# Layer 0 attention, a two-half software pipeline: the seam between the halves is placed ahead of the chunk matrices instead of behind the masks

## The chip, the cores and the metric

The kernel runs on one core of a Trainium2 chip. The metric is the device time of one execution in microseconds (us). It is one program of several phases; the change touches only the first large one, the attention of layer 0.

## The reference, cut to what matters

```python
x = L0_attn_x                                   # (8, 512, 128): 8 batches of 512 rows
h = _layernorm(x) * (1 + ca) + sa
q, k, v, w = ...                                # 16 heads of 8 channels; w: conv, silu, normed
C = einsum('bhtd,bhsd->bhts', w, w) * beta[:, :, None, :]
L = where(tri_s, C, 0.0) + eye(T)
Rhs = where(tri_s, einsum('bhtd,bhjd->bhtj', w, k), 0.0)
A = solve_triangular(L, Rhs, lower=True, unit_diagonal=True)
qw = where(tri, einsum('bhid,bhtd->bhit', q, w), 0.0)
S = einsum('bhid,bhjd->bhij', q, k) - einsum('bhit,bhtj->bhij', qw, beta[..., None] * A)
logits = S * scale + (G[..., :, None] - G[..., None, :])   # G: cumulative log gate
P = softmax(where(tri, logits, -1e30))
x = x + ga * (einsum('bhij,bhjd->bhid', P, v) @ Wo)
# then: 16 experts, top 4; a second layer of attention and a spiking network
```

The triangular solve is done as products of reflections: within chunks of 16 rows step by step ("distances" 1 to 15), between chunks by one 8x8 matrix per head and chunk.

## The kernel before

**Order of the work.** The attention goes through the 8 batches one after the other. A batch is worked on in two halves. Each of the five engines (SP, POOL, ACT, DVE, PE) has its own `front` and `back` generator, and `weave` merges them at build time: each piece is preceded by a `yield` of a due time in arbitrary units, the piece with the smallest due time is emitted next, and at equal due times `back` goes first. What comes out is a fixed instruction list for each engine, which the engine takes in order; semaphores join the engines. The program has nine stages: the front half of batch 0 alone, seven woven stages (the back half of batch b with the front half of batch b+1, a loop body that is executed seven times), and the back half of batch 7 alone. Between two stages all engines report on `over`, SP clears the semaphores and gives `go` (`close`, L288 to 292).

**Front half, in order.** *Preparation* (due 0 to 44): layer norm, the projections, convolution, sigmoid and silu by Exp, Ln and reciprocal with their table loads on ACT, `qf`, `K0`, `wf`, `bw`, the gate's cumulative sum `gdec`; SP then spreads `gdec` by 16 DMAs into `gshift`. *Distances* d = 1 to 15 (due 50 + 4.5 (d - 1)): DVE makes products `tU`, `tX`, `tS` (L642, L646, L630), PE sums them over a head (L867, L872, L858), DVE multiplies again (L659, L662), POOL subtracts from `K0` and `X2` (L322, L326), on which the next distance waits. *Tokens and chunk matrices* (due 116 to 137): PE transposes `bw` and `X2` (L881, L885), ACT copies them out as `bwt`, `at_even`, `at_odd`; PE builds 14 matrices in four `QUADS` (L896, L901), DVE masks them into `Mk` and `Mq` (L672). *Rolling* (due 139 to 152), n = 1 to 7: three groups of small products on PE (L914, L920, L927), copied out by ACT into `Kr` and `turned_m` (L452, L455) and by DVE into `Rr` (L679); each step needs the one before. *Masks* (due 150 to 158): two more products into `Kx`, then on ACT `aux_l`, four `Kxm`, four `aux_g`, four `Kxm` (L463 to 476), on POOL four `Km` (L343) and `vown`; `vm` on DVE (L685).

**Back half, in order.** *Own block* (due 0 to 3): PE transposes `Sd` (L961), DVE adds the mask into `Sdt` (L692), takes its maximum `mown` (L696), swapped by PE into `mpart`. *Maximum jobs* (due 4 to 44): ten groups of four; PE fills four PSUM banks with scores (L982 with L992 on the diagonal, L986 off it), DVE reduces each bank (L704), and the next group needs the banks. `Qm` on ACT after 16 jobs. *Row maximum and own probabilities* (due 48 to 70): a chain on DVE (L710 to 727) and PE, `Qsm` on POOL (L353), Exp on ACT (L487), then 16 spreads on PE (L1020), each multiplied by DVE (L749) and added by POOL (L365). *Scores* (due 70 to 120): 14 groups of up to three jobs of the 40; PE computes scores (L1033, L1042, L1045), ACT takes Exp (L497), PE multiplies by the values (L1056). *Output* (due 123 to 130): L1074, L1078, L762 to 769, L1084, L1088, L774, L780.

**Buffers.** The front half uses PSUM banks 0 to 3 with its own preparation, distances, matrices and rolling; the back half uses banks 4 to 7. `mats` (14 T columns, T = 512) holds the preparation's temporaries and then the matrices; `Pt`, `oi`, `pv` have memory of their own.

## Time and profile before

| | |
|---|---|
| runs | 3: 3684.28, 3689.19, 3691.18 us; median 3689.19 |
| profiled execution | 3705.26 us, its span 3703.5 us |
| PE busy | 2337.3 us, 63% of the span |
| PE loading weights | 1458.0 us, 39% |
| DVE busy | 1749.8 us, 47% |
| ACT busy | 904.7 us, 24% |
| POOL busy | 875.9 us, 24% |
| mean granted clock of PE | 0.700 of full speed |
| attention of layer 0 | from 66.0 to 2145.9 us |

Times are from the span's start. A line such as L704 is line 704 of the kernel. PE is the engine of matmuls, PEld its weight loads, which lie beside PE. In the rows below, a window row gives the stretch, its length, each engine's busy time with its count of instructions, the granted clock as a share of full speed, and the DMA share and rate. A timeline row gives start, duration, engine, line, operation, the written and read tiles with their shape, the count, and in brackets the idle time before it and what ended that.

### The profile page before, as it was taken

The page shows a single profiled execution, that of the slowest core. Times are in us where ns is not written, and L with a number is a line of the kernel's source. Part 1 is how long each engine was busy: PE and PEld are TensorE (multiplying, and loading weights), DVE is VectorE, ACT ScalarE, POOL GpSimd, SP SyncE. Part 2 cuts the span into 40 slices and gives each one's busy share as a digit, 9 for nine tenths or more (in the row PEclk, how much of TensorE's full clock was granted, in tenths as well). Part 3 has the DMA queues.
Part 4 walks back from the last instruction along what each step waited for, and adds up shares of the span by engine and source line. Part 5 has one row for each costly group of instructions (what it writes and reads, how often), then busy time and mean ns, then how long its engine had stood idle before and what let it go on. Part 6 is the DMA issues. An engine that isn't in the chain of part 4 may idle for free. (4 is left out here: it accounts for less than half of the span.)

```text
span 3703.5 us, 41014 instructions
## 1 busy us (share of the span) xinstructions
PE 2337.3 (63%) x15566; PEld 1458.0 (39%) x15566; DVE 1749.8 (47%) x3402; ACT 904.7 (24%) x1800; POOL 875.9 (24%) x892
## 2 busy tenths in 40 slices
PE   3677878779778778787787852079921133444433
PEld 2353544625525536245255452079920011111111
DVE  4537346264374463652743233023322566766666
ACT  1021231222222312312221210046610222222222
POOL 0404204113032041141230104755567000000000
PEclk7757868759678577587695655589965566666666
DMA  2000000000000000000000050122211100000000
GB/s 74 6 1 6 1 3 4 1 6 1 1 6 1 1 6 1 6 1 1 6 1 1 1 204 30 50 67 71 71 47 49 32 0 0 0 0 0 0 0 23
DMA packets 68043, 72.42 MB, mean 20 GB/s; under 512 B 13906, under 2 KB 57858, under 8 KB 66594
## 3 DMA queue, kind: packets, MB, share of 16 engines
q1 hardware_dynamic: 59682, 53.15, 4.4%
q0 software_dynamic: 8192, 16.79, 1.5%
q8 instruction: 133, 2.18, 0.2%
q14 instruction: 36, 0.29, 0.0%
HBM read 34.83 MB, written 30.93 MB: 18 GB/s over the span
## 5 line engine op out<-in xcount | busy, mean ns | idle before, releaser
L497 ACT ACTIVATE a_Pt<-ps 128x512 f32<-128x512 f32 x320 | 168.6, 598 | 582.7 <-PE ps L1042 436.2
L704 DVE TENSOR_REDUCE a_mpart<-ps 128x4 f32<-128x512 f32 x320 | 202.2, 681 | 176.0 <-PE ps L992 106.2
L1292 ACT ACTIVATE b_hid<-ps,b_stage 128x128 f32<-128x128 f32 x576 | 164.2, 368 | 290.0 <-PE ps L1500 290.0
L982 PE MATMUL ps<-a_aux_g,a_g_hotb 24*128 24x512 bf16 (+1 forms) x320 | 134.9, 540 | 83.1 <-DVE a_mpart L704 79.8
L310 POOL TENSOR_TENSOR a_tS<-a_qf,a_K 128x512 f32<-128x512 f32 x8 | 10.4, 1295 | 729.2 <-DVE a_K L585 729.2
L872 PE MATMUL ps<-a_txy,cst 128*128 128x480 f32 (+14 forms) x480 | 165.8, 476 | 24.8 <-DVE a_txy L646 24.6
L1247 POOL COPY b_stage<-b_w 128x1028 f32 x144 | 150.1, 1043 | 125.2 <-PE ps L1509 125.2
L1857 PE MATMUL ps<-c_num,c_wb 128*128 128x512 f32 x128 | 80.5, 716 | 156.9 <-DVE c_num L1776 156.9
L1411 DVE COPY b_hTp<-ps 128x128 f32<-128x128 f32 x144 | 42.0, 291 | 268.0 <-PE ps L1492 155.6
L322 POOL TENSOR_TENSOR a_K<-a_K,a_yU 128x480 f32<-128x480 f32 (+14 forms) x120 | 83.7, 697 | 358.8 <-DVE a_yU L659 358.8
L326 POOL TENSOR_TENSOR a_X<-a_X,a_txy 128x960 f32<-128x960 f32 (+14 forms) x120 | 149.1, 1242 | 73.1 <-DVE a_txy L662 72.3
L1238 POOL DMA_INDIRECT rows_h<-b_htok,b_slot x128 | 125.8, 983 | 144.3 <-DVE b_slot L1391 102.8
L867 PE MATMUL ps<-a_tU,cst 128*128 128x480 f32 (+14 forms) x240 | 104.9, 524 | 86.9 <-DVE a_tU L642 44.0
L1500 PE MATMUL ps<-b_hTp,b_stage 128*128 128x128 f32 x1152 | 153.3, 276 | 0.0
L1509 PE MATMUL ps<-b_stage,b_hid 128*128 128x128 f32 x1152 | 152.4, 275 | 0.3 <-ACT b_hid L1292 0.3
L1492 PE MATMUL ps<-cst,b_hrow 128*128 128x128 f32 x144 | 40.0, 278 | 176.7 <-DMA b_hrow<-rows_h 176.6
L1845 PE MATMUL ps<-cst,c_xn 128*128 128x128 f32 x64 | 17.8, 433 | 204.8 <-DVE c_xn L1721 204.8
L1257 POOL DMA_INDIRECT b_w<-rows_y,b_slot x128 | 130.7, 1021 | 47.1 <-issue 40.6
L1500 PEld LDWEIGHTS ps<-b_hTp,b_stage 128*128 128x128 f32 x1152 | 141.2, 193 | 0.0
L1509 PEld LDWEIGHTS ps<-b_stage,b_hid 128*128 128x128 f32 x1152 | 140.2, 192 | 0.6 <-ACT b_hid L1292 0.5
L872 PEld LDWEIGHTS ps<-a_txy,cst 128*128 128x128 f32 x480 | 95.4, 226 | 86.4 <-DVE a_txy L646 50.0
L982 PEld LDWEIGHTS ps<-a_aux_g,a_g_hotb 24*128 24x128 bf16 (+1 forms) x320 | 24.7, 97 | 245.2 <-DVE a_mpart L704 210.8
(405 smaller groups left out, 5314.8 us busy)
## 6 DMA issues: line engine op xcount, KB each, us to landing
rows_h<-b_stage SPq DMA_DIRECT2D x9, 1024.0 KB, 10.8
b_hrow<-rows_h SPq DMA_DIRECT2D x144, 64.0 KB, 1.9
rows_y<-b_orow SPq DMA_DIRECT2D x144, 64.0 KB, 1.5
b_w<-in_wexp SPq DMA_DIRECT2D x16, 514.0 KB, 16.7
rows_h<-b_htok,b_slot POOLq DMA_INDIRECT x128, 2.2
b_w<-rows_y,b_slot POOLq DMA_INDIRECT x128
out<-xs SPq DMA_DIRECT2D x1, 2048.0 KB, 8.7
cst<-in_const SPq DMA_DIRECT2D x1, 1865.5 KB, 8.2
```

Of the source, the lines that this page charges most:

```text
L326: nc.gpsimd.tensor_tensor(x, x, yX[:, :, 0:n].rearrange("p a (c s) -> p a c s", c=NC), ALU.subtract).then_inc(e_uX.sem, 1)
L497: nc.scalar.activation(Pt[:, n % (2 * LANES), :], ps[:, 4 + n % LANES, :], ACT.Exp).then_inc(e_exp.sem, 1)
L704: nc.vector.tensor_reduce(mpart[:, i, j, 4 * g:4 * g + 4], ps[:, 4 + n % 4, :].rearrange("p (r j) -> p r j", r=4), AX.X, ALU.max).then_inc ...
L867: mm(ps[:, 0, 0:n], con("block8"), tU[:, 0:n], start=True, stop=True).then_inc(e_pU.sem, 1)
L872: last = mm(ps[:, 1 + a, 0:n], con("block8"), tX[:, a, 0:n], start=True, stop=True)
L982: mm(banks[g], g_hotb[some[g], :], aux_g[some[g], :, keys], start=True, stop=False, skip_group_check=True)
L1238: nc.gpsimd.indirect_dma_start(hrows, bass.IndirectOffsetOnAxis(slot[:, k, n:n + 1], 0), htok[:, n, :], None).then_inc(e_sent.sem, 16)
L1247: nc.gpsimd.tensor_copy(stage[:, p % 3, :], we[:, bass.ds(e, 1), :]).then_inc(e_stage.sem, 1)
L1257: nc.gpsimd.indirect_dma_start(got[:, b % 2, t, k, :], None, yrows, bass.IndirectOffsetOnAxis(slot[:, k, n:n + 1], 0))\
L1292: last = nc.scalar.activation(hid[:, p % 2, f, :], ps[:, p % 2, 128 * f:128 * f + 128], ACT.Gelu, bias=stage[:, p % 3, AT_B1 + f:AT_B1 + f ...
L1500: last = mm(ps[:, q % 2, 128 * f:128 * f + 128], stage[:, q % 3, 128 * f:128 * f + 128], hTp[:, q % 2, :], start=True, stop=True, skip_gro ...
L1509: last = mm(ps[:, 4 + r % 2, 0:D], hid[:, r % 2, f, :], stage[:, r % 3, F + D * f:F + D * f + D], start=f == 0, stop=f == NF - 1, skip_gro ...
```

## The change

The generators are cut at another place. `front` ends with the last distance and `Sd`; tokens, matrices, rolling and masks open `back`. They work in PSUM banks 4 to 7, ahead of the maximum jobs. The own block's transposes, mask, maximum and swap no longer open the half: they are put between the rolling steps n = 1, 2, 4 and 5, and the gate's `aux_l` and `aux_g` on ACT ahead of the copy of step 6. The first group of maximum jobs waits for `aux_g`, `Km` and `Kx` but no longer for all of `Kxm`; the fifth group (the first off the diagonal) waits for `Kxm`.

Due times: a distance every 6.6 units (`DS`) instead of 4.5, rolling at 22 + 2.6 n (`RO`, `RS`), all that was in the back half is 38 later (`BK`). The preparation's due times stay. So within a woven stage the preparation is merged with tokens, matrices and rolling; distances 1 to 6 with the maximum jobs; 7 to 9 with the own probabilities; 10 to 15 with score groups 0 to 11; score groups 12 and 13 and the output have no front piece due beside them.

Memory: the preparation gets `prep` (11 T columns, `sq` and `inv` share), `turned_m` its own; `Pt`, `raws`, `oi`, `pv` move into `mats`; `bwt`, `at_even`, `at_odd` into `shared`. The front half gets waits ahead of writing `vf`, `K0`, `bw`, `X2` and `gspl`, which the back half now still reads; the waits for `e_x`, `e_max`, `e_osum`, `e_mulv` and `e_pv` at its end are gone. A stage is over when the distances are.

The diff, cut to its core (what is left out are bank numbers, 0 to 3 becoming 4 to 7, `BK +` ahead of the back half's other due times, and repetitions of the edits shown):

```diff
+        prep = sb("prep", [128, 11 * T])
+        cut = [prep[:, T * i:T * i + T] for i in range(11)]
+        sq = inv = cut[0:3]
+        conv, esig, gate1, w0, ebeta, gy, gabs, gmin = cut[3:11]
         mats = sb("mats", [128, 14 * T])
-        cut = [mats[:, T * i:T * i + T] for i in range(14)]
-        sq, inv = cut[0:3], cut[3:6]
-        conv, esig, gate1, w0, ebeta, gy, gabs, gmin = cut[6:14]
...
-        turned_m = tS[:, 0, :].rearrange("p (i k f) -> p i k f", i=2, k=2)
+        turned_m = sb("turned_m", [128, 2, 2, 128])
...
-        Pt = sb("Pt", [128, 2 * LANES, T])
+        Pt = mats[:, 0:2 * LANES * T].rearrange("p (n t) -> p n t", t=T)
         on, oT, yg = Pt[:, 1, :], Pt[:, 2, :], Pt[:, 0, :]
-        raws = [shared[:, 7 * T + T * i:8 * T + T * i] for i in range(3)] + [Pt[:, 0, :]]
-        oi, pv = sb("oi", [128, T]), sb("pv", [128, 2, T])
+        raws = [mats[:, 6 * T + T * i:7 * T + T * i] for i in range(4)]
+        oi, pv = mats[:, 10 * T:11 * T], mats[:, 11 * T:13 * T].rearrange("p (a t) -> p a t", a=2)
...
+        e_sdT, e_sdm, e_mi, e_miT, e_mic = ev("sdT", 2), ev("sdm", 2), ev("mi"), ev("miT"), ev("mic")
...
+        DS, RO, RS, BK = 6.6, 22, 2.6, 38
...
+                if over_back:
+                    po.wait_ge(*e_tok(1))
...
-                    yield 50 + 4.5 * (d - 1) + 3
+                    yield 50 + DS * (d - 1) + 3
...
-                yield 119
-                po.wait_ge(*e_uU())
-                po.wait_ge(*e_uX())
-                if over_back:
-                    po.wait_ge(*e_x())
+            def back():
+                yield 0
+                nc.gpsimd.tensor_copy(vown[:, :], vf[:, :]).then_inc(e_vown.sem, 1)
                 nc.gpsimd.tensor_copy(steps_k(), in_steps(K0[:, :])).then_inc(e_diag.sem, 1)
-                if over_back:
-                    po.wait_ge(*e_max())
-                    po.wait_ge(*e_qm())
-                    po.wait_ge(*e_qsm())
                 nc.gpsimd.tensor_copy(steps_q(), in_steps(X2[:, 0, :])).then_inc(e_diag.sem, 1)
-                yield 150
-                if over_back:
-                    po.wait_ge(*e_osum())
                 for r in range(4):
                     nc.gpsimd.tensor_scalar(Km[:, r, :], K0[:, :], con("head_of4")[:, r:r + 1], None,
                                             ALU.mult).then_inc(e_km.sem, 1)
-                if over_back:
-                    po.wait_ge(*e_mulv())
-                nc.gpsimd.tensor_copy(vown[:, :], vf[:, :]).then_inc(e_vown.sem, 1)
-
-            def back(after_front):
-                yield 48
+                yield BK + 48
...
-            po.wait_ge(*e_km())
-            po.wait_ge(*e_vown())
+            po.wait_ge(*e_uU())
+            po.wait_ge(*e_uX())
...
+                if over_back:
+                    act.wait_ge(*e_vown())
+                    act.wait_ge(*e_tok(2))
...
-                yield 120
+            def back():
+                yield 1
                 act.wait_ge(*e_tok(0))
-                act.wait_ge(*e_uX())
-                nc.scalar.copy(bwt, ps[:, 0, :].rearrange("p (t f) -> p t f", t=NT)).then_inc(e_tokc.sem, 1)
+                nc.scalar.copy(bwt, ps[:, 4, :].rearrange("p (t f) -> p t f", t=NT)).then_inc(e_tokc.sem, 1)
...
-                    yield 137 + 2.2 * n
+                    yield RO + RS * n
+                    if n == 6:
+                        act.wait_ge(*e_auxp())
+                        nc.scalar.activation(aux_l[:, :], ps[:, 7, :], ACT.Identity, bias=con("one_rows")).then_inc(e_auxl.sem, 1)
+                        act.wait_ge(*e_auxl())
+                        for r in range(4):
+                            nc.scalar.activation(aux_g[:, r, :], aux_l[:, :], ACT.Copy,
+                                                 scale=con("row_of4")[:, r:r + 1]).then_inc(e_auxg.sem, 1)
                     act.wait_ge(*e_pk(n - 1))
                     nc.scalar.copy(Kr[:, n, :].rearrange("p (t x) -> p t x", x=128)[:, :, 0:C * n],
...
+                yield RO + RS * 7 + 2.5
                 act.wait_ge(*e_kx(0))
-                nc.scalar.copy(Kx[:, 0:2, :], ps[:, 0, 0:256].rearrange("p (n s) -> p n s", s=128)).then_inc(e_kxc.sem, 1)
+                nc.scalar.copy(Kx[:, 0:2, :], ps[:, 4, 0:256].rearrange("p (n s) -> p n s", s=128)).then_inc(e_kxc.sem, 1)
                 act.wait_ge(*e_kx(1))
-                nc.scalar.copy(Kx[:, 2, :], ps[:, 1, 0:128]).then_inc(e_kxc.sem, 1)
-                act.wait_ge(*e_auxp())
-                nc.scalar.activation(aux_l[:, :], ps[:, 3, :], ACT.Identity, bias=con("one_rows")).then_inc(e_auxl.sem, 1)
+                nc.scalar.copy(Kx[:, 2, :], ps[:, 5, 0:128]).then_inc(e_kxc.sem, 1)
                 act.wait_ge(*e_kc())
-                if over_back:
-                    act.wait_ge(*e_osum())
...
-                act.wait_ge(*e_auxl())
-                for r in range(4):
-                    nc.scalar.activation(aux_g[:, r, :], aux_l[:, :], ACT.Copy,
-                                         scale=con("row_of4")[:, r:r + 1]).then_inc(e_auxg.sem, 1)
                 act.wait_ge(*e_kxc())
                 for r in range(4):
...
-            def back(after_front):
-                yield 26
+                yield BK + 26
...
+                if over_back:
+                    ve.wait_ge(*e_diag())
+                    ve.wait_ge(*e_km())
...
+                if over_back:
+                    ve.wait_ge(*e_tok(0))
...
+                if over_back:
+                    ve.wait_ge(*e_auxp())
...
-                yield 118
+                yield 50 + DS * 14 + 7
...
+            def back(gate, tiles):
+                yield 3
+                ve.wait_ge(*e_tok(2))
+                nc.vector.tensor_copy(vm[:, :, 0:DH], ps[:, 6, :].rearrange("p (n c) -> p n c", c=DH)).then_inc(e_vm.sem, 1)
                 for j, (kind, n) in enumerate(BUILD):
-                    yield 122 + 1.1 * j
+                    yield 6 + 1.1 * j
...
-                    yield 137 + 2.2 * (7 - r)
+                    yield RO + RS * (7 - r)
                     w = C * (7 - r)
+                    if r in (6, 5):
+                        h = slice(2 * (6 - r), 2 * (6 - r) + 2)
+                        ve.wait_ge(*e_sdT(6 - r))
+                        nc.vector.tensor_tensor(Sdt[:, h, :], ps[:, 7, :].rearrange("p (t e) -> p t e", e=256),
+                                                con("mask_intra").unsqueeze(1).broadcast_to([128, 2, 256]),
+                                                ALU.add).then_inc(e_sdm.sem, 1)
+                    if r == 4:
+                        ve.wait_ge(*e_sdm())
+                        nc.vector.tensor_reduce(mown[:, :, :], Sdt[:, :, :].rearrange("p t (e h) -> p t h e", h=H),
+                                                AX.X, ALU.max).then_inc(e_mi.sem, 1)
+                    if r == 2:
+                        ve.wait_ge(*e_miT())
+                        nc.vector.tensor_copy(mpart[:, :, 4, :], ps[:, 7, 0:64].rearrange("p (t h) -> p t h", h=H))\
+                            .then_inc(e_mic.sem, 1)
...
-            ve.wait_ge(*e_vm())
+            ve.wait_ge(*e_sd())
+            ve.wait_ge(*e_yX())
...
-                yield 116
+                yield 50 + DS * 14 + 6
                 distance(C - 1)
-                pe.wait_ge(*e_bw())
-                pe.wait_ge(*e_yU())
+            def back():
+                yield 0
                 for t in range(NT):
...
+                for t in range(NT):
+                    last = nc.tensor.transpose(ps[:, 6, 128 * t:128 * t + 128], vf[:, 128 * t:128 * t + 128], con("ident"))
                 last.then_inc(e_tok.sem, 1)
...
-                    yield 121 + 1.1 * done
...
                         pe.wait_ge(*e_tokc())
-                        pe.wait_ge(*e_sd())
+                        pe.wait_ge(*e_vm())
...
-                    yield 137 + 2.2 * n - 1
+                    yield RO + RS * n - 1
                     r = 7 - n
+                    if n in (1, 2):
+                        if n == 2:
+                            pe.wait_ge(*e_sdm(0))
+                        for t in range(2):
+                            for half in range(2):
+                                last = nc.tensor.transpose(ps[:, 7, 256 * t + 128 * half:256 * t + 128 * half + 128],
+                                                           Sd[:, half, 256 * (n - 1) + 128 * t:256 * (n - 1) + 128 * t + 128],
+                                                           con("ident"))
+                        last.then_inc(e_sdT.sem, 1)
+                    if n == 4:
+                        pe.wait_ge(*e_mi())
+                        mm(ps[:, 7, 0:64], con("swap"), mown[:, :, :].rearrange("p t h -> p (t h)"), start=True,
+                           stop=True).then_inc(e_miT.sem, 1)
+                    if n == 5:
+                        pe.wait_ge(*e_mic())
+                        for s in range(3):
+                            mm(ps[:, 7, :], gselb[:, s, :], gspl[:, s, :], start=s == 0, stop=False, skip_group_check=True)
+                        last = mm(ps[:, 7, :], step_selb[:, :], stepb[:, :].unsqueeze(1).broadcast_to([8, NT, 128]), start=False,
+                                  stop=True, skip_group_check=True)
+                        last.then_inc(e_auxp.sem, 1)
                     if n >= 2:
                         pe.wait_ge(*e_kc(n - 2))
...
-                yield 153
-                pe.wait_ge(*e_gsp())
-                for s in range(3):
-                    mm(ps[:, 3, :], gselb[:, s, :], gspl[:, s, :], start=s == 0, stop=False, skip_group_check=True)
-                last = mm(ps[:, 3, :], step_selb[:, :], stepb[:, :].unsqueeze(1).broadcast_to([8, NT, 128]), start=False,
-                          stop=True, skip_group_check=True)
-                last.then_inc(e_auxp.sem, 1)
+                yield RO + RS * 7 + 1.5
...
-            def back(after_front):
-                yield 0
-                if after_front:
-                    pe.wait_ge(*e_auxg())
-                    pe.wait_ge(*e_km())
-                    pe.wait_ge(*e_kxm())
-                    pe.wait_ge(*e_vm())
-                for t in range(NT):
...
-                last.then_inc(e_sdT.sem, 1)
-                yield 2
-                pe.wait_ge(*e_mi())
-                mm(ps[:, 6, 0:64], con("swap"), mown[:, :, :].rearrange("p t h -> p (t h)"), start=True,
-                   stop=True).then_inc(e_miT.sem, 1)
-                pe.wait_ge(*e_sdm())
...
-                    yield 4 + 1.1 * n
+                    yield BK + 4 + 1.1 * n
                     i, _, j = MJOBS[n]
                     keys, blk = slice(128 * j, 128 * j + 128), 128 * i
                     if n == 0:
-                        pe.wait_ge(*e_mic())
+                        pe.wait_ge(*e_auxg())
+                        pe.wait_ge(*e_km())
+                        pe.wait_ge(*e_kxc())
+                    if n == NT * G4:
+                        pe.wait_ge(*e_kxm())
```

## Rows read from the trace of the kernel before

**Rows 1.** Windows (columns in the head line): the first stage, front half alone; then all woven stages.
```profile
core 0: us, PE busy (x) PEld busy (x) DVE busy (x) ACT busy (x) POOL busy (x), PEclk, DMA share, GB/s
66.00:106.20 40.20, 18.23 (x28) 5.92 (x28) 22.27 (x33) 20.68 (x27) 3.80 (x3) 0.65 0.02 5
106.20:174.90 68.70, 47.91 (x120) 23.81 (x121) 37.28 (x77) 0.00 (x0) 30.13 (x30) 0.78 0.02 5
174.90:202.00 27.10, 16.75 (x136) 10.19 (x135) 9.43 (x15) 1.85 (x3) 7.89 (x7) 0.50 0.00 1
202.00:230.00 28.00, 27.94 (x142) 27.81 (x143) 2.93 (x8) 4.95 (x14) 0.00 (x0) 0.55 0.00 1
230.00:240.40 10.40, 2.35 (x14) 1.30 (x12) 0.74 (x2) 7.96 (x16) 0.00 (x0) 0.69 0.00 0
...
240.40:1990.90 1750.50, 1405.15 (x10416) 816.24 (x10416) 863.78 (x1526) 428.33 (x742) 405.59 (x420) 0.74 0.01 3
```

**Rows 2.** Windows: one woven stage cut into six stretches.
```profile
240.40:317.60 77.20, 58.57 (x356) 23.43 (x356) 52.22 (x83) 22.91 (x31) 7.09 (x6) 0.59 0.03 7
317.60:362.00 44.40, 33.59 (x78) 15.05 (x79) 30.78 (x47) 2.07 (x2) 27.21 (x27) 0.87 0.00 0
362.00:423.00 61.00, 57.13 (x680) 34.96 (x681) 23.23 (x55) 20.48 (x39) 15.73 (x22) 0.89 0.01 2
423.00:453.40 30.40, 21.60 (x224) 15.59 (x223) 13.61 (x27) 2.83 (x5) 7.90 (x7) 0.81 0.01 1
453.40:480.00 26.60, 26.60 (x141) 26.59 (x142) 2.63 (x7) 4.84 (x13) 0.00 (x0) 0.57 0.00 1
480.00:490.90 10.90, 2.65 (x16) 1.48 (x13) 1.04 (x2) 8.09 (x17) 0.00 (x0) 0.80 0.01 4
```

**Rows 3.** Windows: the last stage, back half alone.
```profile
1991.20:1997.50 6.30, 2.64 (x12) 2.11 (x13) 3.30 (x3) 0.00 (x0) 0.00 (x0) 0.50 0.00 0
1997.50:2046.40 48.90, 40.78 (x312) 15.69 (x312) 24.84 (x40) 2.56 (x4) 0.00 (x0) 0.50 0.00 1
2046.40:2072.30 25.90, 19.57 (x49) 8.90 (x49) 14.86 (x28) 2.07 (x2) 15.72 (x19) 0.74 0.00 1
2072.30:2133.90 61.60, 59.58 (x632) 31.09 (x632) 2.07 (x3) 21.07 (x40) 0.27 (x1) 0.59 0.01 1
2133.90:2145.90 12.00, 8.03 (x56) 7.28 (x52) 4.18 (x12) 0.58 (x1) 0.00 (x0) 0.78 0.00 0
```

**Rows 4.** Timeline: first instruction of the first woven stage and of the last stage.
```profile
240.42 1.28 ACT L395 ACT_TABLE_LOAD   x1 [0.59 <-SPq L292]
...
1991.25 1.51 PE L961 MATMUL ps<-cst,a_Sd 128*128 128x128 f32 x6 [7.62 <-SPq L296]
```

**Rows 5.** Timeline: distances 7 and 10 of the first stage open; one late rolling step, next piece.
```profile
145.23 0.45 DVE L642 TENSOR_TENSOR a_tU<-a_wf,a_K 128x288 f32<-128x288 f32 x1
...
158.46 1.19 DVE L642 TENSOR_TENSOR a_tU<-a_wf,a_K 128x192 f32<-128x192 f32 x1 [0.20 <-POOL a_K L322]
...
477.75 1.04 PE L914 MATMUL ps<-a_roll_k,a_mats 128*128 128x112 f32 x8
...
479.98 0.81 PE L933 MATMUL ps<-a_gspl,a_gselb 128*128 128x512 bf16 x3
```

**Rows 6.** Timeline: one group of four maximum jobs, its filling and its reduction.
```profile
2020.64 2.48 DVE L704 TENSOR_REDUCE a_mpart<-ps 128x4 f32<-128x512 f32 x4 [2.17 <-PE ps L986]
...
2023.18 2.31 PE L986 MATMUL ps<-a_shared,a_roll_q 32*128 32x512 f32 x8
```

**Rows 7.** Timeline: Qsm on POOL, and a distance on PE that waited.
```profile
314.19 6.16 POOL L353 TENSOR_SCALAR a_shared<-a_roll_q,cst 128x384 f32<-128x384 f32 x4 [10.91 <-DVE a_mpart L704]
...
330.05 1.83 PE L867 MATMUL ps<-a_tU,cst 128*128 128x448 f32 x2 [6.07 <-ACT a_Sdt L490]
```

**Rows 8.** Timeline, PE: the same 24 value products in a woven and in the last stage.
```profile
417.65 0.86 PE L1056 MATMUL ps<-a_Pt,a_values 128*32 128x128 f32 x24
...
2105.17 1.51 PE L1056 MATMUL ps<-a_Pt,a_values 128*32 128x128 f32 x24
```

146 lines of the change are left out of this document (59 added, 87 removed).

## The prediction

> **What bounds the kernel now.** I read windows first, because the chain of waits names only the program's last phase. The change touches only the attention, so I cut that part of the trace where the kernel itself cuts it. The reader is to see three things. The seven woven stages take 1750.8 us, from the first stage's start to the last one's: 250.1 each [rows 4]. The two halves alone are known as well: the front half takes 174.4 us, in five pieces of 40.2, 68.7, 27.1, 28.0 and 10.4 [rows 1]; the back half 154.7, in pieces of 6.3, 48.9, 25.9, 61.6 and 12.0 [rows 3]. Together 329.1, so weaving hides 79.0. And within a woven stage PE is busy for 1405.15 of 1750.5 us, 80% [rows 1]: it is the engine closest to a bound, but half of the stage's stretches are paced by PE, DVE and POOL handing one tile back and forth.
>
> Where weaving hides nothing is plain in the six stretches of a stage: the rolling (26.6 us, DVE 2.63, POOL 0) and the masks (10.9 us, PE 2.65, ACT 8.09) have no partner [rows 2]. These 37.5 us are what the new seam can win. It also takes a partner away from others.
>
> **What moves, and the two ends of the attention.** The first stage loses tokens, matrices, rolling and masks. It ends at 174.9 plus about 1.6 for the last subtractions, `Sd` and the hand-over, instead of at 240.4: minus 63.9. The last stage gains them. Tokens and matrices are 27.1 [rows 1], plus 1.0 for the third set of transposes, which now stands ahead of the matrices. Rolling is 28.0, PE busy 27.94 of it [rows 1], so each PE instruction put between its steps counts in full: 2.64 for the own block's transposes and swap [rows 3] and some 1.4 for the gate's sums (the first three are 0.81 at the faster clock [rows 5]); 32.0. The products for `Kx` are 2.9, the 10.4 of the masks [rows 1] less some 7.5 of ACT's thirteen scalings: the gate's five now lie beside the rolling, the eight `Kxm` beside the first four groups of maximum jobs. That is 63.0, and the 6.3 of the own block [rows 3] is gone from the head: plus 56.7. Both ends together: minus 7.2. The new halves alone are 110.5 and 211.4.
>
> **One woven stage, piece by piece.** I price each piece as the back half's length alone plus what the front's companion adds, and take the share that companions add from the stage of before.
>
> (a) Preparation beside tokens, matrices, rolling, `Kx`. Before, the preparation (40.2 alone) beside own block and maxima (55.2 alone) made a stretch of 77.2 [rows 1 to 3]: it added 22.0, 55%. The same here: 63.0 + 22.0 = 85. Following the lists instead: PE's busy time is 18.2 + 16.8 + 27.9 [rows 1], 4.0 put into the rolling, 1.0 and the `Kx` products, some 69. To it come stalls that the lists force: QUAD 3's last mask stands on DVE behind the reciprocal of `ebeta` (due 20 against 20.3), and PE waits for all masks before it may do the head sums: some 6; the first mask behind `xn`, the normalisation's chain on ACT now behind three copies, PE waiting for masks of QUAD 1, the end of `Kx`: some 8. 83. The gate's scalings put 3.2 us on ACT ahead of the copy of step 6; at 4.0 us for a step on PE [rows 1] that is covered, at the late step's 2.23 [rows 5] one us of it is not. I take 83; bounds 69 (PE alone) and 103 (nothing hidden).
>
> (b) Ten groups of maxima beside distances 1 to 6. Alone 48.9 [rows 3] and 39.0 (distance 7 opens 39.0 after 106.2 [rows 5]). A group is 2.31 of filling, then 2.48 of reduction [rows 6], four banks and no fifth, so the engines alternate already. With a distance in the same lists the next filling waits for reductions that stand on DVE behind `yX`, which waits for PE's `tX` sums. At 55% it is 70; following the lists I get 79, two groups and one distance costing nearly their sum. 75; bounds 49 and 88.
>
> (c) Row maximum and own probabilities beside distances 7 to 9. Alone 25.9 [rows 3] and 13.2 [rows 5]. Before, distances 1 to 5 stood here. Now `Qsm` (6.16 us on POOL [rows 7]) and distance 6's subtractions are due at the same 86.0, and a tie goes to `back`. So distance 6 ends 6 us late, distance 7's products wait for it on DVE, and on PE they stand ahead of the own block's transposes. The trace shows this knot already, PE idle 6.07 us [rows 7]. 36.5; bounds 26 and 39.
>
> (d) 14 score groups beside distances 10 to 15 (16.4 alone [rows 1, 5]). Before, ten distances stood beside them, 61.0 us and some 3 more for the last group, PE busy 57.13 and the clock granted at 0.89 [rows 2]; alone the groups took 61.6 at 0.59 [rows 3]. So PE bounds this stretch, and it is the clock that made the distances look free: the same 24 value products are 0.86 in the woven stage and 1.51 alone [rows 8], the two levels 2.4 and 1.2 GHz. Four distances fewer take some 8 to 11 us of PE away; the last groups, alone now, give back some 3. 56; bounds 50 and 66.
>
> (e) The output, 12.0 [rows 3], stood beside matrices, 30.4 for both and a last group [rows 2]. Now nothing is left of the front half to put beside it: 12.0. Hand-over 0.6.
>
> Sum 263.1, against 250.1: 13.0 more, seven times, plus 91; with both ends plus 84. A check by another road: the new halves together are 321.9, and to stay at 250.1 weaving must hide 71.8 of the shorter one's 110.5, 65%. Before it hid 79.0 of 154.7, 51%, or 58% of the 136.9 of the front half that had a partner. 51% gives 265.5, 58% gives 258. The reason is balance: before, the halves were 174 and 155; now one is twice the other and carries nearly all of the stage as one serial chain. The waits added ahead of `vf`, `K0`, `bw`, `X2` and `gspl` I price at nothing: POOL's copies and four `Km` end some 9 us into the stage, transposes at 3, the gate's sums before the cumulative sum comes again. Without that cover `K0` would hold POOL's `tS` and DVE's list. SP's 16 DMAs are issued once a stage as before and are wanted at distance 9, far later.
>
> The profiled execution, 3705.3, would be 3789; it lies 16.1 above the median of the runs, and the median becomes 3689.2 + 84 = 3773.
>
> **The clock, row against rule.** In the rolling PE is busy without a gap, 26.60 of 26.6 us, and is granted 0.57 on the mean [rows 2], so it stays at 1.2 GHz for most of it. The Trainium skill (TensorE: Matmul & The Clock Gate, Part 1) says that the default state is throttled and that sustained activity releases it; by that rule alone the rolling would already run at 2.4 GHz, which this trace contradicts, since busy with weight loads and narrow products is evidently not enough here. Whether wide products between the steps raise it is the faster rival.
>
> **The rivals.** *The clock rises (faster).* The preparation's 512 column products between the rolling steps, and distances between the maxima, lift (a) and (b) to 2.4 GHz, as the stretch with distances and spreads had 0.87 [rows 2]. A rolling step is then 2.23 [rows 5] instead of 4.0, less ACT's uncovered scalings: 10 off; matrices 6 off; ten fillings at half of 2.31: 11 off. All of it gives a stage of 236 and 3583. It decides from 12.0 of these 27 us, a stage of 251.1. Against it: preparation beside maxima, just such a mixture, had 0.59 [rows 2]. About 20 of the 27 would give 243 and 3632. Chance 0.22. *No change*, a stage of 251 within 1 us, 12 of the 27: 3689. Chance 0.06. *Everything in series*: (a) to (c) at the walked 85, 79, 39, and scores at 62 since fewer distances keep the clock up: stage 278, plus 185, 3874. For it speaks that two groups and a distance already cost their sum in my walk. Chance 0.15. *The forecast* has 0.57, its own range 3725 to 3820.
>
> **How the numbers follow.** Faster 0.22, same 0.06 (within 0.2%, 7.4 us, is about what a measurement of this kernel can tell from no change), slower 0.72. From 3640, which leaves out the deeper half of the faster rival, to 3860, which leaves out the worse half of the serial one.
>
> **What the new profile would show.** The first stage's end near 176; the last stage some 211 long; woven stages of 258 to 268. First maximum group some 83 us into a stage; ten groups lasting 75; `Qsm` and then a late distance 7; output alone on a quiet chip. I am wrong if the granted clock is above 0.75 in the first 160 us of a stage, or if distances slip between maximum groups without delaying the next filling.

## The result, and the profile after

The changed kernel takes 3785.78 us (median of 4 runs, 3775.70 to 3794.14), the kernel before beside it 3689.53 (4 runs, 3684.28 to 3691.18): ratio 1.0262, 95% interval 1.0235 to 1.029. It is slower by 2.6%, 96 us. The profiled execution is 3794.14 us with a span of 3792.3; before it was 3705.26 and 3703.5, some 16 us above that kernel's median, so its stages are up to 2 us longer than usual.

First the windows of the changed kernel: the first two woven stages in five stretches each, the last stage whole, all woven stages together. They answer to [rows 1 to 3].

```profile
core 0: us, PE busy (x) PEld busy (x) DVE busy (x) ACT busy (x) POOL busy (x), PEclk, DMA share, GB/s
176.94:252.40 75.46, 58.61 (x326) 39.18 (x327) 34.64 (x55) 30.85 (x52) 11.72 (x10) 0.67 0.01 4
252.40:325.10 72.70, 53.60 (x360) 24.28 (x360) 46.51 (x73) 6.46 (x12) 14.15 (x10) 0.77 0.02 5
325.10:365.70 40.60, 27.34 (x70) 13.51 (x70) 25.16 (x45) 2.07 (x2) 23.53 (x27) 0.79 0.00 0
365.70:434.50 68.80, 66.62 (x649) 40.11 (x650) 11.35 (x35) 19.90 (x39) 6.68 (x13) 0.58 0.00 1
434.50:448.20 13.70, 8.50 (x87) 6.76 (x85) 4.21 (x13) 1.76 (x4) 0.14 (x1) 1.00 0.01 2
448.20:524.00 75.80, 55.87 (x384) 38.17 (x384) 34.25 (x55) 32.30 (x55) 11.50 (x10) 0.75 0.02 5
524.00:594.80 70.80, 51.88 (x312) 22.85 (x300) 46.52 (x73) 5.01 (x9) 14.19 (x10) 0.76 0.01 4
594.80:635.40 40.60, 27.34 (x70) 13.51 (x70) 25.19 (x45) 2.07 (x2) 23.52 (x28) 0.79 0.00 0
635.40:690.60 55.20, 52.49 (x649) 31.43 (x650) 11.62 (x35) 20.02 (x39) 6.62 (x13) 0.81 0.01 1
690.60:704.10 13.50, 8.37 (x86) 6.68 (x84) 4.18 (x12) 1.63 (x3) 0.10 (x1) 1.00 0.01 2
...
2031.64:2239.10 207.46, 175.56 (x1340) 102.69 (x1340) 61.67 (x109) 40.95 (x79) 23.90 (x27) 0.60 0.00 1
177.00:2031.60 1854.60, 1442.21 (x10416) 833.87 (x10416) 851.80 (x1533) 427.44 (x742) 391.98 (x420) 0.74 0.01 3
```

The stretches are the prediction's (a) to (e). The seven woven stages take 1854.7 us, 264.9 each, against 250.1 [rows 4]: plus 104. The first stage ends at 176.94 and not 240.42, minus 63.5; the last is 207.5 long and not 154.7, plus 52.8. Together the attention ends 93 us later, and that is the whole difference of the two profiled executions, 88.8 us in their spans; the rest of the program is 4.4 us shorter.

The fourth stretch is what nobody would guess from a mean. The first stage has 649 PE instructions in it in 68.80 us, the next has the same 649 in 55.20. Three of the five windows of these stages agree within 0.4 us, and (b) within 1.9, most of which is where the windows are cut; this one is 13.6 apart, and its granted clock is 0.58 and 0.81. The stages' first instructions on any engine (176.97, 448.06, 704.00, 973.67, 1229.63, 1499.33, 1755.30, and 2031.67 for the last stage) give lengths of 271.1, 255.9, 269.7, 256.0, 269.7, 256.0 and 276.4: slow and fast by turns, four slow and three fast. The last one is 6.7 us longer than the other slow ones because its stretch (a) is, 80.9 us for 74.5, at a clock of 0.66 for 0.73: (a) too has more than one length.

Where in the stretch it happens, windows of 8 us show, from the first score product on: those of the first stage, then those of the next.

```profile
365.12:373.12 8.00, 7.42 (x130) 4.83 (x129) 2.21 (x6) 3.15 (x6) 1.91 (x4) 1.00 0.01 2
373.12:381.12 8.00, 7.09 (x61) 4.75 (x58) 1.92 (x5) 1.58 (x3) 0.51 (x1) 0.55 0.00 0
381.12:389.12 8.00, 8.00 (x93) 4.43 (x95) 0.49 (x1) 1.95 (x4) 0.84 (x1) 0.50 0.01 2
389.12:397.12 8.00, 6.99 (x44) 3.75 (x36) 2.89 (x9) 1.20 (x3) 1.17 (x2) 0.50 0.00 0
397.12:405.12 8.00, 8.00 (x70) 5.29 (x71) 0.26 (x1) 3.15 (x6) 0.38 (x1) 0.50 0.01 2
634.80:642.80 8.00, 7.42 (x130) 4.83 (x129) 2.22 (x6) 3.15 (x6) 1.88 (x4) 1.00 0.01 2
642.80:650.80 8.00, 7.09 (x61) 4.75 (x58) 1.92 (x5) 1.58 (x3) 0.51 (x1) 0.54 0.00 0
650.80:658.80 8.00, 7.00 (x105) 3.46 (x103) 1.23 (x3) 3.12 (x6) 0.84 (x1) 0.82 0.01 2
658.80:666.80 8.00, 7.62 (x87) 4.36 (x87) 2.16 (x8) 2.32 (x6) 1.17 (x2) 1.00 0.01 2
```

Up to the second window both are alike to the instruction: the clock falls from 1.00 to half in both. Then it comes back in one and stays at 0.50 in the other. In the third window PE is the busier where the clock stays low (8.00 against 7.00), in the fourth the less busy (6.99 against 7.62); from 397.12 to 429.12 it is busy without a gap, and the clock stays at 0.50. The same 24 value products as in [rows 8] take 0.86 us at 370.89 and 1.51 at 384.01 in the first stage, and 0.86 at 657.13 in the next.

The second thing to see is in stretch (c), in the timeline of the changed kernel's first stage. The columns are start, duration, engine and line, and in brackets the idle time before and who ended it.

```profile
325.12 0.70 DVE L707 TENSOR_REDUCE a_mrow<-a_mpart 128x64 f32<-128x320 f32 x1
325.19 4.91 POOL L344 TENSOR_SCALAR a_shared<-a_roll_q,cst 128x384 f32<-128x384 f32 x4 [6.05 <-DVE a_mpart L701]
328.72 1.06 ACT L479 ACTIVATE a_Sdt<-a_Sdt 128x1024 f32<-128x1024 f32 x1 [41.05 <-DVE a_Sdt L724]
330.06 0.81 POOL L327 TENSOR_TENSOR a_K<-a_K,a_yU 128x320 f32<-128x320 f32 x1
330.91 1.67 DVE L641 TENSOR_TENSOR a_tU<-a_wf,a_K 128x288 f32<-128x288 f32 x1 [2.23 <-POOL a_K L327]
332.64 1.33 PE L866 MATMUL ps<-a_tU,cst 128*128 128x288 f32 x2 [4.42 <-DVE a_tU L641]
336.53 1.04 PE L1006 MATMUL ps<-cst,a_Sdt 128*128 128x128 f32 x8
...
341.17 1.01 ACT L482 COPY a_Sdt<-ps 128x1024 f32<-128x1024 f32 x1 [11.39 <-DVE a_mres L733]
342.32 5.77 PE L1016 MATMUL ps<-a_Sdt,cst 128*128 128x512 f32 x8 [4.75 <-ACT a_Sdt L482]
```

That is the knot of [rows 7] on a longer way. The back half's masks of the own queries (L344) hold POOL; behind them stands distance 6's subtraction (L327); distance 7's product on DVE (L641) and on PE (L866) wait for it; and the back half's own blocks (L1006), whose data ACT had ready at 329.78 (L479), stand on PE behind distance 7 until 336.53. From the row maximum to the first spreading product (L1016) it takes 17.2 us, twice with PE idle for more than 4.

### The profile page after: what moved, and what is told of

It is laid out like the page before. It is cut to its first block and busy times, and to the rows that moved or that the text cites. A ratio compares the mean times of both kernels' runs of the same rounds, so it can differ in the third digit from the quotient of the medians.

```text
span 3792.3 us, 41027 instructions
## 1 busy us (share of the span) xinstructions
PE 2374.1 (63%) x15566; PEld 1476.1 (39%) x15566; DVE 1737.5 (46%) x3410; ACT 904.3 (24%) x1800; POOL 866.4 (23%) x892
## 5 line engine op out<-in xcount | busy, mean ns | idle before, releaser
L489 ACT ACTIVATE a_mats<-ps 128x512 f32<-128x512 f32 x320 | 168.6, 597 | 525.1 <-PE ps L1038 378.7
L327 POOL TENSOR_TENSOR a_K<-a_K,a_yU 128x480 f32<-128x480 f32 (+14 forms) x120 | 83.6, 697 | 697.7 <-DVE a_yU L658 697.7
L1016 PE MATMUL ps<-a_Sdt,cst 128*128 128x512 f32 x256 | 133.9, 673 | 41.2 <-ACT a_Sdt L482 35.9
L866 PE MATMUL ps<-a_tU,cst 128*128 128x480 f32 (+14 forms) x240 | 120.1, 593 | 50.4 <-DVE a_tU L641 49.7
L658 DVE TENSOR_TENSOR a_yU<-a_bw,ps 128x480 f32<-128x480 f32 (+14 forms) x120 | 50.1, 418 | 204.3 <-PE ps L866 204.3
L871 PEld LDWEIGHTS ps<-a_txy,cst 128*128 128x128 f32 x480 | 110.0, 260 | 80.9 <-issue 39.6
## 6 DMA issues: line engine op xcount, KB each, us to landing
rows_h<-b_stage SPq DMA_DIRECT2D x9, 1024.0 KB, 10.8
```

Of the source, the lines that this page charges most:

```text
L489: nc.scalar.activation(Pt[:, n % (2 * LANES), :], ps[:, 4 + n % LANES, :], ACT.Exp).then_inc(e_exp.sem, 1)
L871: last = mm(ps[:, 1 + a, 0:n], con("block8"), tX[:, a, 0:n], start=True, stop=True)
L1016: mm(ps[:, 4 + d % LANES, :], con3("spread", 8)[:, d % 8, :], Pd[:, d // 8, :], start=True, stop=True).then_inc(e_rep.sem, 1)
```

## The experiments

Two theories at first. The forecast's: the loss is that of balance, since one half carries nearly all of the stage as a serial chain; then it comes with where the seam lies and no order of the lists gives it back. The rival: it is what two particular places cost, the knot in (c) and the clock in (d). Each ratio is to runs of the kernel before beside it on the same chip, with its 95% interval. Differences between two experiments are of their medians; their chips are not all the same, and the kernel before took 3688 to 3694 us on them.

**1. A wide product in every score group.**
```diff
+ mm(ps[:, 4 + n % LANES, :], identb[:, :], ident4b, start=True, stop=True)
  some = slice(32 * g, 32 * g + (32 if i == j else 24))
```


> Adds one full-width product (128 x 128 by 128 x 512, its result overwritten at once) ahead of each of the 40 score jobs of a stage; nothing else changes. Theory (the granted clock alone makes the score stretch 68.8 us in one stage and 55.2 us in the next, and it is low because the narrow score and distance products leave the array mostly idle): the granted clock is over 0.85 in the score stretch of every stage, the 271/256 us alternation of stages is gone, the stretch takes 54 to 60 us in all of them though it holds 8.5 us more of products, and the time is 3740 to 3770 us. Rival (the two lengths come from something else, such as where distances and fillings fall against each other, or wide products do not hold the clock): the alternation stays, each stage is 8.5 to 17 us longer, and the time is 3845 to 3900 us.

Measured: 3834.18 us, ratio 1.0407 (1.0383 to 1.043). A window of its score stretch in the first stage (the second's is the same, 70.10 us at 0.90):

```profile
364.20:434.30 70.10, 68.19 (x722) 35.63 (x721) 11.27 (x34) 21.08 (x40) 6.32 (x12) 0.90 0.00 1
```

All seven are so: the turns are gone, as the theory had it. The time is neither theory's, because the added products were mis-priced: from the start of one to the next product on PE it is 346 ns on the mean (13.5 us for 39 of them; their own records overlap the next and are 413 ns long), so forty take 13.9 us, not 8.5. Without them the stretch is 70.1 - 13.9 = 56.2, near the fast 57.0. So the clock makes the difference. Forty wide products cost in a slow stretch what they release, and in a fast one 13 us more.

**2. The order of four steps at the knot.** The own queries' masks go behind distance 6 on POOL, the own blocks ahead of distance 7 on PE and DVE.
```diff
-                yield BK + 48      # POOL, masks of the own queries
+                yield BK + 48.5
-                yield BK + 52      # ACT, exponentials
+                yield BK + 50.5
-                yield BK + 54      # PE and DVE, own blocks
+                yield BK + 51
```


> The changed kernel with four due times moved: GpSimd's masks of the own queries behind distance 6 and not ahead of it, the own blocks' turns and their masks ahead of distance 7, ScalarE's exponentials 1.5 earlier. Theory (the order of the queues around the row maximum makes that stretch 40.6 us where 36.5 was forecast): the stretch from the row maximum to the first score falls to 33 to 36 us, and the time to 3730 to 3760 us. Rival (what this stretch has is TensorE's work at its clock, the order only moves where it waits): 39 to 42 us as now, and 3775 to 3795 us.

Measured: 3678.03 us (9 runs), ratio 0.9972 (0.9962 to 0.9982): 108 us less than the changed kernel, and 0.3% under the kernel before, a difference clear of the noise but small. Both theories are off; the stretch does what the first said, and far more comes with it. Windows of its first stage, (a) to (d), then the seven stages:

```profile
174.96:250.40 75.44, 58.61 (x324) 39.15 (x325) 34.66 (x55) 30.82 (x52) 11.70 (x10) 0.67 0.01 4
250.40:323.15 72.75, 53.61 (x360) 24.30 (x360) 46.52 (x74) 6.47 (x12) 16.14 (x12) 0.77 0.02 5
323.15:358.50 35.35, 27.04 (x70) 13.86 (x70) 23.61 (x45) 2.07 (x2) 21.59 (x27) 0.81 0.00 0
358.50:413.10 54.60, 51.79 (x682) 31.09 (x682) 11.61 (x35) 21.07 (x40) 6.60 (x13) 0.87 0.01 2
...
174.96:1933.30 1758.34, 1375.35 (x10416) 809.80 (x10417) 842.88 (x1533) 428.24 (x742) 391.77 (x420) 0.79 0.01 3
```

(a) and (b) are the same as in the changed kernel's first stage to 0.1 us. (c) is 35.35 instead of 40.60. And (d) is 54.6 at a clock of 0.87, in all seven stages: its slow kind does not occur. A stage is 251.2. But turns remain, in another stretch: (a) is some 75 us in three stages and 78.5 in four. Here are a long and a short one, with 0.70 and 0.75; the first stage has 0.67 and is short all the same, so that the clock makes this difference is not shown.

```profile
673.65:752.25 78.60, 58.44 (x327) 42.02 (x328) 34.46 (x55) 31.06 (x52) 11.60 (x10) 0.70 0.01 4
1431.45:1506.05 74.60, 53.92 (x328) 38.02 (x330) 34.38 (x55) 30.96 (x52) 11.62 (x10) 0.75 0.01 4
```

The seven stages together are 96 us shorter than the changed kernel's: 37 from (c) and 71 from (d), less 12 by which (a) and (b) grew. The timeline of this kernel in (c) shows the own blocks no longer behind the distance:

```profile
327.59 1.97 PE L1006 MATMUL ps<-cst,a_Sdt 128*128 128x128 f32 x8 [1.61 <-ACT a_Sdt L479]
...
332.16 1.30 PE L866 MATMUL ps<-a_tU,cst 128*128 128x288 f32 x2 [2.60 <-ACT a_Sdt L482]
```

The own blocks stand at 327.59, 4.4 us behind the row maximum and not 11.4, and the first spreading product (336.24) comes 13.1 us behind it, not 17.2.

**3. The seam behind the rolling.** Of all that was moved, only masks, auxiliary rows and rotated keys are moved.
```diff
@@ GpSimd, the kernel before
-                yield 150
                 for r in range(4):   # Km, then the copy of v
+            def back(after_front):
+                yield 0
@@ TensorE: gate's sums and the products for Kx
-                yield 153
+            def back(after_front):
+                yield 0
```


> The kernel before with the seam moved the other way: behind the rolling, so that matrices and rolling stay the alone end of the half that prepares, and only the masks, the rotated keys and the auxiliary rows (10.9 us alone) open the half that scores, beside the next stage's preparation. Theory (a part is worth bringing over only as far as it leaves TensorE and the clock room; masks are VectorE's and ScalarE's work beside a stretch that TensorE leaves half idle): 5 to 9 us of each stage's 10.9 are hidden, and the time is 3630 to 3660 us, faster than before. Rival (every item taken over comes back in full as a later end, as the matrices and the rolling did): 3685 to 3700 us. Third (the masks delay the preparation's own copies): 3700 to 3740 us.

Measured: 3660.26 us, ratio 0.993 (0.9913 to 0.9946): 0.7% under the kernel before, at the edge of the theory's 3630 to 3660. A stage is 245.0 (1715.05 us for seven), 5.1 less than before:

```profile
227.59:1942.64 1715.05, 1402.35 (x10416) 812.64 (x10416) 864.77 (x1526) 428.27 (x742) 405.70 (x420) 0.76 0.01 3
```

**4. The seam between matrices and rolling.**
```diff
-        DS, RO, RS, BK = 6.6, 22, 2.6, 38
+        DS, RO, RS, BK = 5.7, 2, 2.6, 20
@@ TensorE: tokens, then matrices, stay in front(), in banks 0 to 3
-            def back():
-                yield 0
+                pe.wait_ge(*e_bw())
+                pe.wait_ge(*e_yU())
...
-                    yield 5 + 1.1 * done
+                    yield 141 + 1.1 * done
```


> The changed kernel with the seam between the matrices and the rolling: tokens and matrices (27 us alone) stay at the end of the half that prepares, as in the kernel before, and the rolling and the masks open the half that scores; offsets are set anew for it (distances 5.7 apart, the back half's dues 18 earlier). Theory (the loss comes of the tokens and matrices: they share TensorE and VectorE with the preparation's products, and push all fifteen distances' partner behind them; the rolling has idle engines around it, and beside the preparation the clock is 0.67 to 0.75 and not 0.57): a stage takes 243 to 250 us and the time is 3630 to 3700 us. Rival (the rolling itself is the cost, for it is a chain that stretches beside anything, and a back half of 183 us is still far longer than the front's 138): a stage takes 258 to 265 us, the time 3750 to 3790 us.

Measured: 3579.62 us, ratio 0.9713 (0.9689 to 0.9737), below the theory's range. A stage is 235.5 on the mean. One stage in windows: rolling and masks beside the preparation, maxima, row maximum in two parts, scores.

```profile
1151.55:1190.40 38.85, 34.15 (x186) 25.66 (x186) 18.71 (x24) 18.85 (x37) 6.29 (x5) 0.85 0.00 1
1190.40:1264.00 73.60, 53.99 (x342) 21.69 (x342) 44.31 (x68) 15.20 (x22) 12.68 (x9) 0.64 0.03 8
1264.00:1280.80 16.80, 9.27 (x30) 5.42 (x29) 15.53 (x23) 2.07 (x2) 8.31 (x7) 0.82 0.00 0
1280.80:1303.60 22.80, 19.36 (x48) 8.64 (x49) 15.18 (x30) 0.00 (x0) 16.78 (x22) 1.00 0.00 1
1303.60:1359.50 55.90, 54.38 (x742) 34.19 (x742) 17.30 (x44) 22.72 (x43) 10.27 (x17) 0.94 0.01 1
```

Against the first stage of kernel 2, both taken from the first instruction of any engine (1149.84 here, 174.96 there), the opening stretch is 34.8 us shorter (40.6 for 75.4); from the first maximum group to the first score it is 5.0 longer; scores 1.3 longer; output and what follows 22.4 for 11.6, 10.8 longer: 17.7 together, for a stage of 232.1 against 249.8. The matrices cost 10.8 us beside the output and far more at the head of the stage. Rolling and masks, 38.4 alone [rows 1], take 38.85 with part of the preparation beside them, at a granted 0.85, and not the 0.57 of the rolling and 0.80 of the masks in [rows 2]. The edit also sets new distances between the due times, though, and runs 11 and 12 will show that these alone can move this kernel by 3%.

**5 and 6. The two halves of the reordering.** Run 5 has only the first of experiment 2's lines, run 6 only the others.

> The changed kernel with the first of the four moves of the reordered one alone: GpSimd masks the own queries behind distance 6. First theory (both halves of the reordering count: 4.4 us that TensorE waited for distance 7 go with this one, the rest with the other): the stretch from the row maximum to the first score is 37 to 39 us, half of the slow score stretches turn fast, and the time is 3710 to 3760 us. Second (the masks are what held everything): 3670 to 3690 us, as with all four moves. Third (the own blocks' chain behind distance 7 is what counts): 3770 to 3795 us.

> The changed kernel with the other moves alone: the own blocks' turns and masks ahead of distance 7 and ScalarE's exponentials 1.5 earlier; GpSimd's masks stay ahead of distance 6. First theory (both halves count): the stretch is 36 to 39 us and the time 3700 to 3750 us. Second (the masks alone count): 3770 to 3795 us. Third (the own chain alone counts, for it no longer waits for distance 7): 3670 to 3690 us.

Measured: run 5 3727.13 us (7 runs, spread from 3704.59 to 3805.64), ratio 1.0062 (1.0035 to 1.0089); run 6 3685.62 (10 runs), ratio 0.9966 (0.9952 to 0.998). Run 5 is where its first theory had it. Run 6 is the third theory's: the own blocks' place is enough for nearly all of the gain. The two do not add: the masks' place alone brings 59 us, the own blocks' alone 100, both 108. Windows of run 5: the row maximum and then the score stretch of its fourth stage, and the score stretch of the next.

```profile
1086.80:1123.60 36.80, 27.69 (x70) 13.66 (x70) 23.60 (x45) 2.07 (x2) 22.18 (x27) 0.81 0.00 0
1123.60:1194.60 71.00, 68.63 (x682) 40.88 (x682) 11.33 (x35) 21.08 (x40) 6.68 (x13) 0.61 0.00 1
1393.20:1449.80 56.60, 53.91 (x682) 32.50 (x682) 11.64 (x35) 21.07 (x40) 6.67 (x13) 0.82 0.01 1
```

Two of its seven stages are slow and five fast. In the traces the sum closes: (c) is 3.8 us less in seven stages, 27, and two slow stretches fewer, at 14.4, are 29; together 55. The openings (a) are 4.5 us longer in all, the output behind the two slow stretches 3.7, (b) 0.8, and the seven stages come out 46 us shorter. The profiled execution as a whole is 50.7 us under the changed kernel's. The spread of its seven runs, 101 us, would fit from none to seven slow stretches at 14.4 each; the mean granted clock of an execution falls as its time grows (0.726 at 3704.59 us, 0.713 at the profiled 3743.41, 0.695 at 3805.64), but only the profiled execution's stages can be seen. In run 6, (c) is 35.5 and (d) 54.8 in every stage.

**7. The kernel before, reordered.**
```diff
-                yield 48
+                yield 48.5
-                yield 52
+                yield 50.5
-                yield 54
+                yield 51.5
```


> The kernel before with the same four moves (masks of the own queries 0.5 later, exponentials 1.5 earlier, own blocks 2.5 earlier, which puts them at the same place behind a distance). Theory (the collision is made by the changed kernel's offset between the halves, in the kernel before nothing of a distance lies between these steps): 3680 to 3700 us, no change, and all of the reordered kernel's gain belongs to the changed one. Rival (the order was bad before too): 3600 to 3670 us, and the seam as such still costs 30 to 80 us.

Measured: 3690.67 us (10 runs), ratio 0.9992 (0.9978 to 1.0005): no change, as the theory said. So the gain of the reordering belongs to the changed kernel's offset; the theory's reason is that only there a distance comes between these steps.

**8. The best seam, reordered.** Experiment 4's kernel with experiment 2's lines.

> The kernel with the seam between matrices and rolling, and the same four moves (own blocks ahead of distance 5 here). Theory (its stretch from the row maximum to the first score, with 22.8 us from the first spreading product to the first score as in the changed kernel, has the own chain behind a distance as well): 2 to 5 us of each stage go, 3545 to 3570 us. Rival (its offsets do not collide, the clock in the score stretch is 0.94 already): 3570 to 3590 us.

Measured: 3571.75 us, ratio 0.9695 (0.9641 to 0.9749). Nearer to the rival: its interval overlaps that of run 4, so the 8 us between them are not shown. Its median is the lowest of the study all the same, 3% under the kernel before.

**9. Products in the gap ahead of the spreads.**
```diff
                 last.then_inc(e_mT.sem, 1)
+                for n in range(10):
+                    mm(ps[:, 5 + n % 2, :], identb[:, :], ident4b, start=True, stop=True)
```


> The changed kernel with ten full-width products (128 x 128 by 128 x 512, their results unused) on TensorE behind the turned row maximum, where it idles 4.7 us for distance 7; all waits and the order of the queues stay. Theory (it is the idle stretch ahead of the score products that leads to the low clock in them): no score stretch of 69 to 71 us is left, and the time is 3720 to 3750 us. Rival (what the engine did ahead of the score stretch has no bearing, since it is 325 to 366 us alike in both kinds of stage, at a granted clock of 0.79): slow and fast score stretches stay, about half and half, and the time is 3775 to 3800 us.

Measured: 3737.74 us (5 runs), ratio 1.0108 (1.0072 to 1.0145): 48 us less than the changed kernel, with more work in it. But the turns are not gone. Its score stretches are of two kinds, four of the first and three of the second; two windows:

```profile
362.20:425.80 63.60, 61.18 (x682) 36.20 (x682) 11.55 (x35) 21.08 (x40) 6.58 (x13) 0.71 0.01 1
...
894.60:949.40 54.80, 51.91 (x682) 31.36 (x682) 11.62 (x35) 21.08 (x40) 6.66 (x13) 0.88 0.01 1
```

So what happens ahead of the stretch matters to the clock in it, against the rival; it does not alone decide it. Whether it is the products or the time is not separated: with them the first spreading product comes 15.9 us behind the row maximum and not 17.2, so the scores begin 1.3 us earlier.

**10. A wide product in every third score job.** As in experiment 1, under `if n % LANES == 0`, 14 a stage.

> The changed kernel with one full-width product (result overwritten at once) ahead of every third score job, 14 in a stage and not 40. Theory (dense products among the narrow ones keep the clock up, and 14 do it as the 40 did, for 14 x 0.41 = 5.8 us and not 16.5): score stretches of 59 to 61 us in every stage, a stage of 260 to 262 us, 3750 to 3775 us. Rival (14 are too few): some score stretches stay slow, at 73 to 76 us, and the time is 3790 to 3840 us.

Measured: 3721.67 us, ratio 1.0082 (1.0065 to 1.0099), 64 less than the changed kernel and below the theory's own range. One of its score stretches:

```profile
369.50:426.00 56.50, 54.14 (x696) 32.03 (x695) 11.26 (x34) 21.07 (x40) 6.33 (x12) 0.88 0.01 1
```

All seven are so. Fourteen products whose results nobody reads take 14 us off every slow stretch, and a fast one is no longer for them (57.0 in the changed kernel from the first score to the output's first product). That is the plainest sign that the clock, not the amount of work, makes the slow kind.

**11 and 12. The spacing of the distances in kernel 8.** `DS` 5.1 and 6.3 for 5.7; in run 11 also `BK + 50.3` for `BK + 51`.

> The reordered kernel with the seam between matrices and rolling, its distances due 5.1 apart and not 5.7 (own blocks' dues 0.7 earlier, to stay between distances 4 and 5). Theory (the preparing half ends last there, its matrices run 24 us behind the output's first product, so an earlier distance 15 brings the matrices beside the scores): the stage ends 3 to 6 us earlier, 3530 to 3555 us. Rival (the distances then sit closer beside the ten maximum groups, which are walked in series with them): 3570 to 3600 us.

> The same with its distances due 6.3 apart. Theory of the run before: the matrices end 3 to 6 us later behind the output, 3590 to 3620 us. Rival: the maximum groups pass faster and the scores have the distances beside them, 3545 to 3570 us.

Measured: run 11 3680.06 us (3633.53 to 3697.11, too far apart for a ratio); run 12 3657.35, ratio 0.9898 (0.9869 to 0.9927). Run 12 goes the way its theory said and further: from the output's first product to the seam it is 31.6 us on the mean and not kernel 8's 22.4, and the stage 246.5 for 231.7, 14.9 longer where 3 to 6 were expected. Run 11 was to be faster and is slower: its first two stages are 235.4 and 236.7, the five after them 252.3 to 252.6, and the score stretch of a late one has lost the clock, against the second stage's:

```profile
592.45:649.30 56.85, 53.63 (x735) 32.90 (x735) 15.51 (x42) 22.72 (x43) 8.32 (x15) 0.91 0.01 1
1084.20:1152.90 68.70, 65.47 (x734) 40.47 (x734) 15.49 (x42) 22.92 (x43) 8.34 (x15) 0.73 0.01 1
```

That is 68.7 us at 0.73, where its own second stage has 56.9 at 0.91 and kernel 8 has 55.9 at 0.94. Of the 21 us by which the late stages are longer than kernel 8's, 12.8 are this stretch; some 3 are the opening, and 2 to 6 the maximum groups, which is what the rival named. Spacing the distances 0.6 closer, with the own blocks' due 0.7 earlier, thus cost 3% of the program, more than half of it where the clock was lost. It also says something of the comparisons above: in this kernel 0.6 units of spacing either way move the time by 86 to 108 us, as much as the seam's place in experiment 4. How much of a kernel's time is its seam and how much its offsets was not separated; only experiment 3 moves the seam at the old spacing.

## Why the prediction was right, and where it was not

The forecast was slower, 3773 in a range of 3640 to 3860; measured 3786. The sum is within 13 us, and that is luck in part: errors in its terms cancel, and the reason given for them was not the one that decides.

**The ends.** First stage 110.9 long, forecast 110.5; last stage 207.5, forecast 211.4. Both together minus 10.7, forecast minus 7.2. Right.

**(a)** forecast 83, measured 75.5 and 74.5 in the first two stages (448.06 to the first group at 522.54). The stall at the last mask was as walked: PE idle 5.63 us for it behind the reciprocal, forecast some 6, as the timeline shows:

```profile
210.25 3.35 DVE L558 RECIPROCAL a_prep<-a_prep 128x512 f32<-128x512 f32 x1
213.52 0.63 DVE L675 TENSOR_TENSOR a_mats<-ps,cst 128x512 f32<-128x512 f32 x1
...
214.20 2.08 PE L825 MATMUL ps<-a_prep,cst 128*128 128x512 f32 x2 [5.63 <-DVE a_mats L675]
```

What was mis-sized is the clock behind it. I had left the rolling at 1.2 GHz; beside the preparation it rises. Windows over its first and its second part:

```profile
218.00:234.40 16.40, 13.84 (x69) 12.51 (x69) 10.65 (x13) 7.01 (x13) 1.32 (x1) 0.60 0.00 1
234.40:252.40 18.00, 15.65 (x101) 12.16 (x101) 6.12 (x10) 12.65 (x24) 2.40 (x2) 0.92 0.04 13
```

The second part has 0.92. So the faster rival's mechanism is there. With (b) it brings some 10 of the 27 us that it could, if all that these stretches are under the forecast is put down to the clock: short of the 12 from which it would have decided.

**(b)** forecast 75, measured 72.7 and 72.3. Right within its bounds. The mark that I set, a clock above 0.75 in the first 160 us, was met in none of the seven stages, with 0.70 in the first and 0.74 in the second as its two ends; but 0.74 is too near the mark to prove anything.

**(c)** forecast 36.5, measured 40.6. The knot was named in the prediction, place and engines. It was priced 4 us too low, because I followed it only to the own blocks and not through their chain: PE's turns, ACT's copy, then the spreads. Untied, it is 35.4, so the knot costs 5.2 us, and the 36.5, in which it was meant to be contained, left only 1.1 for it.

**(d)** is the step that failed, though its number looks harmless: "it is the clock that made the distances look free", and "14 score groups, 56; bounds 50 and 66". Measured from the first score to the output's first product: 57.0 in three stages, 70.7 in four, mean 64.8. I took one value of a quantity that has two. The 56 is the fast kind; the slow kind lies above my bound. My walk had the parts for it, [rows 3] with 61.6 us at 0.59 for these groups alone, but I blended the clocks into a mean instead of asking which of them each stage would get.

**The sum.** Per stage (a) and (b) were some 10 us too dear, (c) and (d) 13 too cheap, and output with hand-over, 12.6 forecast, came to some 11. Errors that have nothing to do with each other cancelled; the stage came to 264.9 against 263.1.

**The reason.** The prediction said: "The reason is balance: before, the halves were 174 and 155; now one is twice the other". Experiments 2, 6 and 7 refute it as an explanation of the loss by itself. With the same seam and the same unequal halves, moving a few steps by 0.5 to 3 of the planner's units gives back 108 us, all of the loss and 0.3% more. What the reordering takes away is a collision (5 us a stage) and a clock lost in four score stretches of seven (14 to 16 us each). What the halves alone and the weaving do can be counted: the first stage, taken from 66.0 on (its true start lies between 65.0 and 66.0), and the last stage are the halves alone, and their sum less a woven stage is what weaving hides.

```
kernel                alone: front + back = sum    a stage   hidden
before                174.4 + 154.7 = 329.1        250.1     79.0
changed               110.9 + 207.5 = 318.4        264.9     53.5
changed, reordered    109.0 + 199.2 = 308.2        251.2     57.0
seam behind rolling   161.6 + 156.7 = 318.3        245.0     73.3
seam behind matrices  134.1 + 172.6 = 306.7        235.5     71.2
```

The unequal halves do hide 22 us less. But the prediction took the sum as given, and it is not: moving matrices, rolling and masks makes the halves alone up to 22 us shorter. I put that down to masks, gate, own block and rolling standing beside each other within one half; no run isolates it. Part of it is the clock again: the score stretch of the last stage is 61.6 us at 0.59 before, 57.4 at 0.67 in the reordered kernel and 55.6 at 0.72 with the seam behind the matrices. In the reordered kernel the two cancel. With the seam behind the matrices the same is saved in the sum and only 8 are lost in hiding. So, at the offsets that were tried, the seam had a good place behind the matrices (3% under the kernel before), a fair one behind the rolling (0.7%) and a neutral one ahead of them all, and the changed kernel was at the neutral one with the collision and the lost clock on top.

What stays open: what makes the clock come back in one stage and not in the next, when both are the same up to the fall; and whether reordering keeps the clock by the order of the work or by its time. The turns, fast after slow, suggest that a stage's own length shifts where the fall meets the work; no run tests that.

## What to carry to other kernels

When two halves are woven by due times, cut a loss into stretches before blaming the cut itself: a stretch with the same instructions and two lengths is not about work at all. Look at any step whose data is ready early and that stands in an engine's queue behind the other half's late one; with the offset between the halves, this changes even where no line of it was edited. And forecast the clock as one of two levels for each stretch and stage, with a price for each, never as a mean. A due time moved by half a unit can change it.

## What the runs showed of the hardware

The granted clock fell and stayed at 0.50 in windows where PE was busy for 8.00 of 8 us (381.12 and 397.12), among narrow products (most of them of 32 rows) and their weight loads. With fourteen full-width products a stage, beside the stretch's 682 PE instructions, it was 0.88, and the program 64 us shorter; with forty it was 0.90, but they took 0.35 us each and cost more than they gave. In the reordered kernel the opening stretch has two lengths as well, but its mean clock does not order them: 75.4 us at 0.67 in the first stage, 74.6 at 0.75 and 78.6 at 0.70 in later ones. The Trainium skill (TensorE: Matmul & The Clock Gate, Part 1) says that activity releases the throttle; these rows agree only if activity is not the same as PE's busy time in the profile.

Times spread with the clock: run 5, whose profiled execution has both kinds of score stretch, ranges over 101 us in 7 runs, the longest with the lowest mean clock, and run 2, whose profiled score stretches are all fast, over 11 us in 9.
